# Shifted cross attention: the mask added by GpSimd in the returned product, one query stack

## The reference, cut to what matters

```python
qh = (q @ w_q) ...; kh = (k @ w_k) ...; vh = (v @ w_v) ...          # q = layernorm(x), k = v = ctx
ph = (pe @ w_p).reshape(2 * s, N_HEADS, D_K).transpose(1, 0, 2)
ac = einsum('bhtd,bhsd->bhts', qh + b_u, kh)
bd = left_shift(einsum('bhtd,hmd->bhtm', qh + b_v, ph))              # zero where j - i > M - L
scores = where(mask, (ac + bd) / sqrt(D_K), -inf)                    # mask: the same [256, 256] for all batches and heads
x = x + (softmax(scores) @ vh) @ w_o
```

## Time and profile before

| | |
|---|---|
| median of 3 runs | 2078.66 us (2072.72 to 2079.03) |
| the profiled execution's own time | 2087.96 us |
| its span | 2086.2 us, 39703 instructions |
| granted TensorE clock, mean | 0.921 of full speed |
| DMA | 228.54 MB, mean 110 GB/s |
| L1 cross attention | about 686 to 985 us of the span |

### The profile page before, as it was taken

One profiled execution on the slowest core, in us unless ns is written; L12 is line 12 of the kernel. 1 busy time (PEld: TensorE's weight loads), 2 busy tenths in 40 slices (PEclk: granted clock), 3 DMA queues, 4 the chain that ended last, 5 costly groups with the idle time before them and its releaser, 6 DMA issues.

```text
span 2086.2 us, 39703 instructions
## 1 busy us (share of the span) xinstructions
PE 1720.5 (82%) x14024; PEld 1311.1 (63%) x14024; DVE 1455.4 (70%) x5662; ACT 1035.3 (50%) x2588; POOL 461.5 (22%) x448
## 2 busy tenths in 40 slices
PE   6588999999998678879998687899868868765886
PEld 5455687776776445546887465555548856554775
DVE  6689524777877578778888777778875466567643
ACT  3277525666765556656333354456434435531343
POOL 3300110000002000000556200000364544213442
PEclk9899999999999789989999799899979989976998
DMA  5334067000001978885200333323125543242356
GB/s 179 79 75 115 16 243 230 1 1 1 1 1 31 280 214 233 250 215 165 81 1 19 94 76 90 76 65 96 47 73 182 165 132 93 71 147 79 97 163 203
DMA packets 211053, 228.54 MB, mean 110 GB/s; under 512 B 16052, under 2 KB 179276, under 8 KB 210216
## 3 DMA queue, kind: packets, MB, share of 16 engines
q1 hardware_dynamic: 205864, 215.71, 36.1%
q0 software_dynamic: 4992, 10.30, 1.4%
HBM read 130.57 MB, written 94.98 MB: 108 GB/s over the span
## 4 chain that ended last, share of the span: by engine, by line
PE 47%; DVE 26%; DMA 9%; ACT 7%; issue 4%; POOL 3%; SPq 2%; another core or an unknown queue 1%; DVEq 0%; ACTq 0%; POOLq 0%
PE banks L746 40%; ACT P L1509 4%; DVE P L1993 4%; PE banks L1059 3%; DMA stacks<-region 2%; DMA back<-mask,block_to 2%; DVE region L1915 2%; SPq L2684 2%; DVE P L1835 2%; DVE route L1835 1%; DVE P L2092 1%; DVE region L2162 1%; PE banks L1151 1%; ACT region L1509 1%; DVE skew_room L1835 1%
## 5 line engine op out<-in xcount | busy, mean ns | idle before, releaser
L2508 POOL TENSOR_TENSOR norms<-norms,consts 128x2 f32<-128x2 f32 x112 | 81.5, 728 | 1224.5 <-DVE norms L1839 1223.9
L1509 ACT ACTIVATE P<-P,negm 128x256 f32<-128x256 f32 x512 | 240.5, 499 | 109.2 <-DVE negm L2112 64.6
L1509 ACT ACTIVATE P<-banks 128x512 f32<-128x512 f32 (+2 forms) x392 | 188.4, 511 | 162.5 <-PE banks L746 155.2
L1509 ACT ACTIVATE region<-banks 128x384 f32<-128x384 f32 (+4 forms) x221 | 108.5, 506 | 80.7 <-PE banks L746 58.8
L746 PE MATMUL banks<-xnT,region 128*128 128x256 f32 x544 | 139.3, 390 | 3.4 <-ACT xnT L1509 3.3
L746 PE MATMUL banks<-kz,qs 128*128 128x256 bf16 (+1 forms) x512 | 112.0, 280 | 34.8 <-DVE negm L1993 14.2
L746 PE MATMUL banks<-region 64*128 64x256 f32 (+6 forms) x922 | 126.7, 364 | 8.9 <-ACT region L1509 3.5
L746 PE MATMUL banks<-qv,region 128*128 128x256 bf16 (+2 forms) x512 | 117.6, 270 | 18.2 <-ACT P L1509 13.7
L746 PE MATMUL banks<-qs,kz 128*128 128x256 bf16 (+2 forms) x512 | 117.1, 270 | 16.7 <-ACT P L1509 8.2
L746 PE MATMUL banks<-kz,region 128*128 128x256 f32 x512 | 121.7, 384 | 4.0 <-DVE skew_room L1835 2.8
L2587 POOL DMA_INDIRECT back<-mask,block_to x92 | 89.6, 974 | 111.7 <-DVE mask L2340 100.7
(11 more groups left out here) (292 smaller groups left out, 4465.4 us busy)
## 6 DMA issues: line engine op xcount, KB each, us to landing
stacks<-region SPq DMA_DIRECT2D x178, 192.0 KB, 3.0
sorted<-qs SPq DMA_DIRECT2D x4, 4160.0 KB
skew<-region SPq DMA_DIRECT2D x64, 256.0 KB
qs<-stacks SPq DMA_DIRECT2D x24, 384.0 KB
kz<-stacks SPq DMA_DIRECT2D x48, 192.0 KB
skew<-region SPq DMA_DIRECT2D x64, 128.0 KB
skew_room<-skew SPq DMA_DIRECT2D x32, 256.0 KB
P<-skew SPq DMA_DIRECT2D x32, 256.0 KB
```

The lines of the kernel that those rows point to most:

```text
L1509: return a.e.activation(o, i, f, **kw)
L2508: g.e.tensor_tensor(room[:, :, 0], room[:, :, 0], pows[:, :], ALU.pow).then_inc(done, 1)
```

## The change

- The identity products of the shifted cross attention are gone. GpSimd gets main work in that stage: when a pair's lane is back, it adds the mask (bfloat16) into the returned columns, two additions per pair (2 x 128 and 2 x 256 columns), and signals `mask_added`; VectorE waits for that in place of `lane_in`. The columns behind the diagonal are set to the mask once instead of to zero.
- The stack qv is gone, with its drain, cut and transfers. The shift uses qs. What b_v has over b_u enters as three more rows of the products: ones in qs (set by VectorE in the stage before, in both rooms), and in phz the pieces of (b_v - b_u) ph / sqrt(8), computed once in the first stage and put there by two small transfers.
- qs now has two rooms in this stage (the old qs and qv). Its pieces go out and come back in the slot of the old qv; the key's return still waits for the last item's heads.
- GpSimd's order string is new; the other engines' strings are as they were, and the steps keep their number (empty yields stand where steps went).

```diff
@@ tensor_program, L0_attn @@
+            if (s.n, j) == (0, 3):
+                p.wait_ge(tables, GAP)
+                p.wait_ge(scalar_tables, PLACE)
+                mm(s.T[0:H, 0:S], gap_of_heads, place).then_inc(first_full, 1)
+                p.free[s.n, "T"] = (tables, GAP_CUT)
@@ tensor_program, L1_xattn @@
-            p.wait_ge(place_sem, 64)
-            p.wait_ge(tables, IDENTB)
-            p.wait_ge(tables, MASK)
+            p.wait_ge(place_sem, 96)
+            p.next(s.mask_added, PAIRS)
...
-                    i = mm(s.S1[:, t * S + far:(t + 1) * S], qv[:, h // 2, t * 128:(t + 1) * 128], phz[:, h % 2, h // 2, far:])
+                    i = mm(s.S1[:, t * S + far:(t + 1) * S], qs[:, h // 2, t * 128:(t + 1) * 128], phz[:, h % 2, h // 2, far:])
...
-                    p.wait_ge(s.stack_in, back_before(j) + 64)
+                    p.wait_ge(s.stack_in, back_before(j) + 48)
...
-                        mm(o, qs[:, now // 2, t * 128:(t + 1) * 128], kz[:, now % 2, now // 2, :], True, False)
-                        i = mm(o, identb[:, :], L1x_mask[:, t, :], False, True)
+                        i = mm(o, qs[:, now // 2, t * 128:(t + 1) * 128], kz[:, now % 2, now // 2, :])
@@ scalar_program, split_k @@
-                    a.wait_ge(s.stack_out, 32 * (stacks_before(j) + stacks_of(j) - 1))
+                    a.wait_ge(s.stack_out, 32 * (stacks_before(j) + 1))
@@ vector_program, front @@
-                if bv is not None:
-                    q_drained(bank, bv, s.natural_qv)
                 q_drained(bank, bq, s.natural_q).then_inc(s.q_out, 1)
-                if bv is not None:
-                    yield from q_pieces(s, j, s.natural_qv, 0)
-                yield from q_pieces(s, j, s.natural_q, 0 if bv is None else 1)
+                yield from q_pieces(s, j, s.natural_q)
+                if j // ITEMS == 4:
+                    yield
                 yield from split_k(s, j)
@@ vector_program, table (j == 0) @@
+                step(red(gap_of_heads.rearrange("p (a i) -> p a i", a=2), ident.rearrange("p (a d i) -> p a i d", a=2, d=DH), ALU.add))
+                step(tt(gap, P["L1x_vb"], P["L1x_ub"], ALU.subtract))
+                ts(gap_of_heads, gap_of_heads, gap, DH ** -0.5, ALU.mult, ALU.mult).then_inc(tables, 1)
@@ vector_program, L0_attn @@
+            if (s.n, j) == (0, 3):
+                v.wait_ge(first_full, GAP_FULL)
+                T = s.T[0:H, 0:S]
+                step(v.e.tensor_copy(gap_cut[:, 0, :], T))
+                step(tt(gap_rest, T, gap_cut[:, 0, :], ALU.subtract))
+                step(v.e.tensor_copy(gap_cut[:, 1, :], gap_rest))
+                tt(gap_cut[:, 2, :], gap_rest, gap_cut[:, 1, :], ALU.subtract).then_inc(tables, 1)
@@ vector_program, L1_attn @@
+            v.wait_ge(place_sem, 80)
+            if j == 3 * ITEMS + 2:
+                v.wait_ge(skew_zero, 288)
+                for room in s.qs_of[4]:
+                    i = v.e.memset(room[AUG:AUG + 3], 1.0)
+                i.then_inc(s.rooms_clean, 1)
@@ vector_program, L1_xattn @@
-                    v.wait_ge(s.lane_in[now // 2 % 2], v.next(s.lane_in[now // 2 % 2], 32 if now % 2 == 0 else 0))
+                    v.wait_ge(s.mask_added, v.next(s.mask_added, 1 if now % 2 == 0 else 0))
@@ gpsimd_program @@
+        def L1_xattn(s, b, j):
+            for pair in range(PAIRS):
+                slot = pair % 2
+                yield
+                g.wait_ge(s.lane_in[slot], g.next(s.lane_in[slot], 32))
+                for t in range(TOK):
+                    near = 128 + 128 * t
+                    part = s.skewed[slot][:, :, t, 0:near]
+                    i = g.e.tensor_tensor(part, part, L1x_mask[:, t:t + 1, 0:near].to_broadcast([128, 2, near]), ALU.add)
+                i.then_inc(s.mask_added, 1)
+                g.next(s.mask_added)
+            yield
@@ sync_program, front @@
-                d.wait_ge(place_sem, 64)
-                yield from stack_out(s, j, 2)
-                yield from stack_back(s, j, 2, [s.qv_of[j % 2][0:AUG]], ROOMS[4][1] if j % 2 else 0)
                 yield from stack_out(s, j, 0)
+                yield from q_back(s, j)
+                yield
                 yield from stack_out(s, j, 1)
                 yield
                 d.wait_ge(s.heads_out, H * (ITEMS + k))
                 d.wait_ge(s.stack_in, back_before(j) + 16)
-                yield from q_back(s, j)
+                yield
                 yield from k_back(s, j)
@@ sync_program, L0_ffn @@
+                d.wait_ge(tables, GAP_CUT)
+                d.wait_ge(place_sem, 64)
+                gap_rows = streams[0].via[2, 0:3 * H * S]
+                dma(gap_rows.rearrange("(k h s) -> h k s", k=3, s=S), gap_cut, place_sem)
...
+                d.wait_ge(place_sem, 80)
+                dma(phz[AUG:AUG + 3].rearrange("p a i s -> p (a i s)"), gap_rows.rearrange("(k m) -> k m", k=3), place_sem)
```

More of the change, by code:

```diff
@@ L501, in __init__ @@
         self.own_var, self.own_rstd = signal("own_var"), signal("own_rstd")
+        self.mask_added = self.own_rstd
         self.loaded = signal("loaded")
@@ L648, in program @@
         s.pieces_of = {n: as_pieces(pieces[n]) for n in FRONTS}
-        s.qs_of = {n: [s.qs[:, :, :], s.qs[:, :, :] if n == 4 else s.qv[:, :, :]] for n in FRONTS}
+        s.qs_of = {n: [s.qs[:, :, :], s.qv[:, :, :]] for n in FRONTS}
         s.kz_of = {n: [s.kz[:, :, :, :], kz2[n].bitcast(BF16).rearrange("p (a i c) -> p a i c", a=2, i=PAIRS) if n in kz2 else s.kz[:, :, :, :]]
@@ L716, in program @@
     MOVED = 16 * TOK * ITEMS
-    def stacks_of(j):
-        return 3 if j // ITEMS == 4 else 2
     def back_before(j):
         m = FRONT_SEQ.index(j)
-        return 48 * m + 16 * max(m - ITEMS, 0)
+        return 48 * m + 16 * max(m - 2 * ITEMS, 0)
     UNITS = [(f, k) for f in range(FT) for k in range(2)]
@@ L804, in stacks_in @@
             yield
[L805 removed]
+            p.wait_ge(s.stack_in, back_before(j) + (48 if j // ITEMS in (1, 4) else 64))
             p.wait_ge(s.f_out, out_before(j) + 2)
@@ L1944, in q_pieces, with front @@
             split_q(s, q, s.pieces_of[n], s.cut)
-        def front(k_bank, bq=None, bv=None, norm_of=None):
+        def front(k_bank, bq=None, norm_of=None):
             def run(s, b, j):
@@ L2448, in front_rope @@
             v.e.tensor_copy(s.natural_q, s.T[:, 0:S]).then_inc(s.q_out, 1)
-            yield from q_pieces(s, j, s.natural_q, 0)
+            yield from q_pieces(s, j, s.natural_q)
             yield from split_k(s, j)
@@ L2624, in front @@
             if j == 4 * ITEMS:
+                g.wait_ge(tables, MASK)
                 for room in s.skewed:
-                    i = g.e.memset(room[:, :, 0, 128:], 0.0)
+                    i = g.e.tensor_copy(room[:, :, 0, 128:], L1x_mask[:, 0:1, 128:].to_broadcast([128, 2, 128]))
                 i.then_inc(s.behind_zero, 1)
@@ L2630, in front @@
                     g.wait_ge(z.x_done, j)
-                g.e.memset(s.qv_of[1], 0.0)
                 clean_v(s.v_of[4][1]).then_inc(s.rooms_clean, 1)
@@ L2718, in q_back @@
             qs = s.qs_of[j // ITEMS][j % 2]
-            yield from stack_back(s, j, 0, [qs[0:AUG]] + ([qs[AUG:AUG + 6]] if j // ITEMS in (6, 7, 9) else []), 0)
+            yield from stack_back(s, j, 0, [qs[0:AUG]] + ([qs[AUG:AUG + 6]] if j // ITEMS in (6, 7, 9) else []),
+                                  ONES_BEHIND if j // ITEMS == 4 else 0)
         def k_back(s, j):
```

49 lines of the change are left out of this document (27 added, 22 removed).

## The result

| | before | after |
|---|---|---|
| median of the runs, us | 2078.85 (4 runs) | 2098.73 (4 runs, 2096.86 to 2105.08) |
| ratio after/before | | 1.0105, 95% interval 1.0082 to 1.0128 |
| profiled execution: span (own time), us | 2086.2 (2088.0) | 2103.3 (2105.1) |
| first to last add of the shifted cross attention, us | 702.0 to 987.0: 285.0 | 711.9 to 1009.2: 297.3 |

The changed kernel is slower by 1.05%, 20 us. The forecast was 9 us faster; the time lies 3 us above the stated range, and 4 above the 2095 us of the rival "lanes set the pace".

A forecast was written before the change was run, and what follows sets the result against it. The shifted cross attention was taken as a mixed bound with no engine full. Terms A to H summed -7 -5 -10 -5 +13 +2 +2 +1 = -9 us, giving a median of 2069.7 us; stated range 2048 to 2096.

The forecast's parts named there:

- lanes set the pace: Rival, shifted cross attention: GpSimd's 2.2 us exceed what a lane can spare on most passes; +16 us, 2095 us, chance 0.23.
- E: Shifted cross attention: GpSimd's two additions put 2.2 us into each lane, paid on six passes; +13 us, bounds +8 and +23.
- A: Shifted cross attention: removing 256 identity products frees 28 us of TensorE, partly on the chain; -7 us, bounds 0 and -28.
- B: Shifted cross attention: VectorE loses the second query stack's drains, casts and subtractions; -5 us, bounds 0 and -24.
- D: Transfer queue, shifted cross attention: half the bytes in front of k's return go; -5 us, bounds 0 and -11.
- G: First stage and L1's self-attention: new small product, small VectorE operations, transfers and memsets; +2 us, bounds 0 and +8.
- F: Shifted cross attention: less TensorE work leaves more gaps, lowering the granted clock by 0.02; +2 us, bounds 0 and +6.
- C: Shifted cross attention: the room for cut pieces is used twice, not three times, per item; -10 us, bounds 0 and -13.
- H: GpSimd and VectorE at one memory: 32 subtractions pay 0.1 us each, PSUM adds none; +1 us, bounds 0 and +3.
- VectorE's adds are slowed: Rival: memory sharing with GpSimd delays VectorE's adds even beside PSUM, 256 x 0.1 us; +16 us, 2095 us, chance 0.04.
- Nothing to see: Rival: what two engines save is waited for on transfers; about -2 us, 2077 us, chance 0.23.
- All comes out: Rival: lanes stay hidden, GpSimd's additions cost +4, products and second stack give 20; -26 us, 2053 us, chance 0.12.

The follow-up runs named there:

- identity_back: Changed kernel with the mask added by identity products again and no GpSimd addition, one query stack kept; 2072.64 us, 0.9985 of the kernel before; repeated: 2079.86 us, 1.0007.
- identity_and_ones: Changed kernel with identity products back, no GpSimd mask additions, and the memsets of ones moved to GpSimd; 2078.25 us, 0.9991 of the kernel before; repeated: 2068.22 us, 0.9952.
- no_mask_at_all: Changed kernel without GpSimd's additions and without identity products, the returned columns' mask addition left out; 2076.77 us, 0.9993 of the kernel before.
- identity_one_tile: Changed kernel without GpSimd additions, with the identity product for the second row tile alone (128 products), first tile's mask left out; 2078.41 us, 1.0001 of the kernel before.
- gpsimd_adds_twice: Changed kernel with GpSimd making its two additions of a pair twice, so the mask is added twice; 2146.07 us, 1.0335 of the kernel before.
- experiment 4: Changed kernel with neither GpSimd's mask additions nor identity products, 0.9993 of the kernel before; its text also counts close lanes in the kernel before's trace.

## Why the prediction was wrong

It was wrong in sign, and the rival that it gave 0.23, lanes set the pace, is what happened. The step that failed is E's count of lanes: six were taken to pay for GpSimd's 2.2 us, and the runs show 19.4 us, the price of 10.6 lanes at 1.83 us, with 39 of 64 lanes close enough to be made late. Without E the change comes out near no change (identity_back, 0.9985 and 1.0007): A gave nothing, B to D half of their sum, and G took most of that. By its steps:

- **A, identity products, -7: failed.** Measured between 1 and 6 us of loss in the stage (identity_back's 271.7 and 273.2, identity_and_ones' 276.9 and 275.3, against 277.9 without), and nothing in the medians (0.9985 and 1.0007 against 0.9993). The step took a third of 28 us of freed issue time to be paid on the chain, because L746 has 55 us there. What was freed was waited for instead. Its bound of 0 with F's of 6 takes this in.
- **F, the clock, +2: mis-sized.** The clock fell by 0.08 to 0.10, not 0.02. A and F were priced as two terms, but they come together: +1 to +6 us in the stage, not -5. From identity_back to no_mask_at_all busy share and clock fell together, from 0.81 and 0.96 to 0.78 and 0.86. The Trainium skill (TensorE: Matmul & The Clock Gate, Why this matters for your kernels) advises to keep TensorE busy without gaps; that pair agrees, but identity_one_tile, busy 0.82 of its stage at a clock of 0.87, shows that the busy share alone does not tell the clock.
- **B, C, D, -20 in sum: right in kind, half in size.** The pieces' transfer out fell from three chain pieces, 12.7 us, to one of 2.99; the chain no longer has a piece of kz; TensorE waits for kz once, 7.8 us, in place of three times, 10.7 us, the longest 8.6. The longest of these waits hardly got shorter. Measured for the three together: the stage from 285.0 to 271.7 to 276.9 in four executions, 8 to 13 us.
- **E, GpSimd in each lane, +13: the step that failed.** The duration was nearly right (1.83 us and 0.07 of hand-over, predicted 2.2 in all), the number of lanes paid was not: 19.4 / 1.83 is 10.6 lanes, where six were taken and "at most once in 3 pairs", 10.7, was the bound. That the kernel sits on that bound is chance, for it is none: in gpsimd_adds_twice 66 us for 3.67 us a lane are 18 lanes. The bound counts 32 pairs, those of one stream, where the stage has 64. The step read the spare 0.5 us correctly in the earlier trace rows and then did not follow it: it took two lanes for the exception, while 39 of the 64 had less than 1.9 us to spare (experiment 4). The Trainium skill (GPSIMD Engine Reference, 3.1) has 4497 ns for 2048 elements, from which 1.7 us plus dispatch were estimated; the trace's 1.83 agrees.
- **G, set-up, +2: mis-sized, at its bound of 8.** A memset took 1.765 us, inside the stated 0.66 to 2.5; what failed is that only 2 us were taken to be paid for all four and the rest. In a stage where TensorE is busy 283 of 290 us and its work waits for VectorE in a fixed order, 7.1 us of memsets cost 6 to 8. The rest of the set-up cost 0 to 4.6 us, 2 on average. The Trainium skill (VectorE: DVE Perf Modes, Zero memsets can be issued as uint32) counts one cycle per element, which by its 0.96 GHz would be an estimate of 2.1 us. The trace has 1.765 us, and the measurement decides.
- **H, two engines at one memory, +1: right, and the rival "VectorE's adds are slowed" is refuted.** The adds take 418 ns with GpSimd busy beside them. The subtractions with two SBUF inputs are held up where they meet GpSimd's additions, by 2.2 us in all, and the one of 824.52 is on the chain with 1.0 us more than its 0.42.
- **The other rivals.** "Nothing to see" had the right view of A and B, that what is freed is waited for, and missed E and G. "All comes out" fell with E.

The sum with the measured terms, in the stage: -13.3 (one stack, 285.0 to 271.7), +6.2 (identity products out, to 277.9), +19.4 (GpSimd in, to 297.3): +12.3. With the 9.9 us ahead of it that is 22.2 us of lag behind the stage, and the medians differ by 20. The terms come from one execution each; the scatter of the stage between like kernels is 1.5 to 3 us, that of its start up to 5.

Of the marks set in advance, GpSimd's busy time (121 us in the stage, near 130 foretold), the nearly missing transfer of the pieces and 15 us of waits pointed to the forecast, the clock below 0.86 and a stage of 297 and not 290 us against it. The mark "VectorE's wait at its adds above 30 us" was badly chosen: the rival came true at 15, since part of the same lateness is booked under other instructions and under those who wait for VectorE.

Not tried: issuing a head's shift more than five heads ahead of its scores, which might give GpSimd room; adding the mask before the transfer out; the gap's set-up on another engine. That 25 us per us at the high end comes from both streams' lanes being paid one after the other on an engine with a fixed order is an argument, not shown.

## What to carry to other kernels

An idle engine is not a free one: work put into a loop with latency (transfer, then add, then the next heads) is paid on the passes that have less to spare than it takes, and the price per microsecond rises with its length, so count the passes that were close (39 of 64 here), not those on the chain (five before). Taking products away where TensorE is not what bounds can return nothing: the time is waited for elsewhere, and the clock fell with it; price both as one term. A small one-off operation on an engine that feeds a full TensorE costs nearly its whole duration there; move it to an engine that nobody waits for.

## What the runs showed of the hardware that was not expected

The granted clock of the stage moved with a little work. With the 256 identity products and no GpSimd addition it was 0.93 to 0.96 in four executions, without them 0.86 and with half of them 0.87, in one execution each. Why half of them bring back so little is open.

A float32 addition of GpSimd with a bfloat16 second input takes 0.674 us for 256 elements and 1.158 for 512: 1.9 ns per element and 0.19 fixed. The plain float32 one of 256 elements takes 0.76; the bfloat16 input is not dearer.

A memset of 2048 columns on 3 partitions takes 1.765 us on VectorE and 1.80 to 1.88 on GpSimd, nearly the same; what differs is who waits.

A subtraction of VectorE with two SBUF inputs (256 columns, 0.42 us alone) took up to 1.43 us where GpSimd added at the same time, and ended 0.3 us behind it, while additions with one PSUM and one SBUF input kept 0.42.
